# A graph network on one core: four groups instead of one per turn of TensorE's loop in the sparse sums

## The reference, cut to what matters

```python
# layer 0: ten hops
for _ in range(10):
    f = 0.9 * segment_sum(f[src] * edge_weight[:, None], dst, n) + 0.1 * feat_0
# layer 1: an edge network on [x[src], x[dst], edge_attr], averaged by destination
# layer 2: degree-normalised sum over edges, a linear layer
agg = segment_sum(x[src] * ci[src][:, None], dst, n) * cj[:, None]
# layer 3: symmetric-normalised sum with self loops, batch norm
agg = segment_sum(h[src] * norm[:, None], dst, n)
```

## Time and profile before

| | |
|---|---|
| median of 3 runs | 9797.47 us (9789.39 to 9800.16) |
| span of the profiled execution | 10,854.4 us (no other time was recorded for it) |
| TensorE matmuls busy | 8603.5 us, 79% of the span, 233,310 of them |
| VectorE busy | 7212.7 us, 66% |
| GpSimd busy | 5092.9 us, 47% |
| ScalarE busy | 4566.9 us, 42% |
| DMA | 1796 MB, mean 165 GB/s |
| packets of the DMA queue for instructions, q8 | 151, 2.47 MB |

### The profile page before, as it was taken

The page is one execution under the profiler, slowest core; times in us unless marked ns, Lnnn a source line. Parts: engine busy times, 40 slices in busy tenths (PEclk is TensorE's granted clock), DMA queues, the critical chain, the costliest instruction groups (busy, mean ns, idle before and its releaser), DMA issues. The chain is left out here.

```text
span 10854.4 us, 564438 instructions
## 1 busy us (share of the span) xinstructions
PE 8603.5 (79%) x233310; PEld 6985.0 (64%) x233310; DVE 7212.7 (66%) x17719; ACT 4566.9 (42%) x9489; POOL 5092.9 (47%) x4838
## 2 busy tenths in 40 slices
PE   5886776788989989889899894777777777759585
PEld 4665665778888888888888882343334333348585
DVE  7998987877777777777777773333333333367377
ACT  2332997954444444444444442333333333324132
POOL 0000000046767667667667674455555555537064
PEclk9998995589999999999999997888888888879598
DMA  3000005588988889889888893222222222249085
GB/s 28 0 0 0 0 0 186 226 278 282 303 280 287 297 283 302 280 282 302 282 287 297 282 302 80 53 57 56 52 53 56 55 54 54 54 138 303 21 289 178
DMA packets 548661, 1796.17 MB, mean 165 GB/s; under 512 B 210662, under 2 KB 272126, under 8 KB 546686
## 3 DMA queue, kind: packets, MB, share of 16 engines
q1 hardware_dynamic: 469374, 1740.04, 48.4%
q0 software_dynamic: 59776, 46.03, 2.8%
q10 hardware_dynamic: 19328, 7.36, 0.4%
HBM read 1628.31 MB, written 159.79 MB: 165 GB/s over the span
## 5 line engine op out<-in xcount | busy, mean ns | idle before, releaser
L1159 POOL TENSOR_TENSOR arena<-arena 128x768 f32<-128x768 f32 (+2 forms) x1800 | 2739.3, 1522 | 3965.3 <-DVE arena L1215 3922.5
L1128 ACT CAST arena<-banks 128x384 bf16<-128x384 f32 (+1 forms) x3600 | 1993.1, 608 | 2856.2 <-DVE banks L1211 2855.1
L1259 PE MATMUL banks<-arena 32*128 32x144 bf16 x118800 | 2359.3, 224 | 188.1 <-issue 173.1
L1247 PE MATMUL banks<-arena 128*128 128x48 bf16 x58800 | 2504.4, 184 | 2.7 <-issue 2.6
L1247 PEld LDWEIGHTS banks<-arena 128*128 128x128 fp8e4 x58800 | 2345.7, 96 | 6.7 <-issue 5.9
L1215 DVE TENSOR_TENSOR arena<-banks,arena 128x384 f32<-128x384 f32 (+1 forms) x3600 | 1931.2, 567 | 568.2 <-ACT arena L1128 568.2
L1247 PE MATMUL banks<-xc,arena 128*128 128x48 bf16 x24500 | 2063.6, 185 | 219.1 <-DVE arena L1186 59.7
L1504 POOL DMA_INDIRECT f<-node_table,idx x1568 | 1537.6, 981 | 1444.1 <-ACT idx L1512 979.2
L1247 PEld LDWEIGHTS banks<-xc,arena 128*128 128x128 fp8e4 x24500 | 1903.0, 96 | 415.4 <-issue 147.4
L1259 PEld LDWEIGHTS banks<-arena 32*128 32x128 bf16 x118800 | 1965.5, 92 | 315.0 <-issue 220.7
L1211 DVE TENSOR_TENSOR banks<-banks,wslot 128x384 f32<-128x384 f32 (+1 forms) x3600 | 1877.1, 567 | 366.8 <-PE banks L1247 363.2
(11 more groups left out here) (329 smaller groups left out, 11611.5 us busy)
## 6 DMA issues: line engine op xcount, KB each, us to landing
arena<-onehots SPq DMA_DIRECT2D x1200, 768.0 KB, 4.2
arena<-onehots SPq DMA_DIRECT2D x300, 864.0 KB, 4.4
arena<-onehots SPq DMA_DIRECT2D x300, 800.0 KB, 4.3
arena<-in_dst SPq DMA_DIRECT2D x195, 512.0 KB
onehots<-arena SPq DMA_DIRECT2D x100, 768.0 KB, 3.3
node_table<-xc SPq DMA_DIRECT2D x11, 2352.0 KB, 17.8
f<-node_table,idx POOLq DMA_INDIRECT x1568
onehots<-arena SPq DMA_DIRECT2D x25, 864.0 KB, 3.5
```

The costliest lines, as they stand in the source:

```text
L1128: m = nc.scalar.copy(as_bank(mp_b[:, b % 3, 0, tiles, :, 1]), bank)
L1159: nc.gpsimd.tensor_tensor(mp[:, b % 3, 2, 0:NTILE[b], :], mp[:, b % 3, 1, 0:NTILE[b], :], mp_b[:, b % 3, 1, 0:NTILE[b], :, 1], ALU.subtrac ...
L1247: m = nc.tensor.matmul(to, hot[:, i * P:(i + 1) * P], x_part, start=c == 0, stop=c == 2)
L1259: m = nc.tensor.matmul(banks[:, 4 + q, 0:3 * D], hot[rows, i * P:(i + 1) * P], mp_b[rows, b % 3, :, i, :, 1], start=b == 0 and i == 0, sto ...
```

## The change

TensorE's loop over the first 24 groups takes four groups in a turn, so that it has 6 turns and a body four times as long, written out. The order of the matmuls and waits is the same. The loops of the other engines keep one group per turn.

```diff
+PE_TURN = 4
...
+    assert (NGRP - 1) % PE_TURN == 0
...
-                    with pe.Fori(0, NGRP - 1) as d:
-                        for b in range(NBATCH):
-                            gather(d + (b + 2) // NBATCH, (b + 2) % NBATCH)
-                            scatter(d, b)
+                    with pe.Fori(0, (NGRP - 1) // PE_TURN) as t:
+                        for d in (t * PE_TURN + i for i in range(PE_TURN)):
+                            for b in range(NBATCH):
+                                gather(d + (b + 2) // NBATCH, (b + 2) % NBATCH)
+                                scatter(d, b)
```

## The result

The changed kernel takes 12,264 us (median of 4 runs, 12,224 to 12,272) against 9,797 us for the kernel before on the same chip. The ratio is 1.2511, with a 95% interval of 1.2496 to 1.2526. The prediction had the direction, the mechanism and the range (10,950 to 12,300); its middle, 11,550, was 714 us too low.

A forecast was written before the change was run, and what follows sets the result against it. TensorE was taken to bound the sums, DMA close behind. Fetching 276 groups (1,352 us) and 60 dearer branches (306 us) gave +1,660 us on 9,797; from three readings it took 11,550 us, range 10,950 to 12,300.

The forecast's parts named there:

- TensorE sets the pace, other engines are covered: Loop over groups in the sums: TensorE is busy 15.45 of 16.10 us a group; slower TensorE covers the others.
- DMA is close behind: Loop over groups: DMA is busy 92% of the 16.10 us turn, 14.8 us a group.
- the third reading to the measured time: Unprofiled loop already at its DMA limit of 14.8 us a group, fetches as long as ever: 11,816 us.
- A turn of before runs from held instructions, the rest is fetched: TensorE's loop: a turn of about 1,400 instructions needs no instruction packets; all other code is fetched, 256 instructions a packet.
- The change saves up to 0.9 us for each branch removed: TensorE's loop edge: 18 of 23 taken branches per sum go, 216 in all, at most 190 us gained.
- The rival in which fetching is hidden: TensorE's unrolled loop: blocks come in time, so the kernel gets 190 us faster, 9,610 us; chance 5%.
- The rival in which a part is kept: TensorE's unrolled loop: some 7 of 22 blocks are met again, +1,130 us, about 10,930; chance 5%.
- 5.46 periods of 3.85 us per group: TensorE's unrolled loop: 5.46 instruction blocks a group, one per period p, 21.0 us a group; 276 groups cost 1,352 us.
- A branch that stays costs 5.1 us more: TensorE's loop: 60 remaining branches jump to blocks not held, 3.6 us plus about 1.5 us each, 306 us.
- The rival with DMA or the clock as the bound: In the sums: packets queue behind one-hots, p 4.34 or more, +2,420 us, 12,220; or pauses lower the clock; chance 10%.
- The sum: Whole kernel: 1,352 us for fetched groups plus 306 us for remaining branches, +1,660 us.
- The three readings from the profile to the measured time: Whole kernel, from a profiled 10,854 to the median 9,797 us: same ratio 11,295, same addition 11,457, or DMA-limited loop 11,816.

The follow-up runs named there:

- experiment 10: Kernel before, with SyncE's loop fetching only 64 columns of each batch of one-hots: 9,765 us against 9,803 on that chip.
- experiment 5: Kernel before with 120 more one-column matmuls per turn of TensorE's loop, a body of about 1,640 instructions: 13,731 us against 10,832 on that chip.
- experiment 9: Kernel with the 1,640-instruction body, plus 48 matmuls ahead of TensorE's loop in each copy of the sum: 10,640 us against 9,803 for before.
- its second form: Kernel with the 1,640-instruction body, with 27 instead of 48 matmuls ahead of the loop in each copy: 11,968 us against 10,852 for before.
- experiment 3: Changed kernel with two groups per turn instead of four: 12,654 us, ratio 1.292 to the kernel before.
- experiment 6: Kernel before with 360 more one-column matmuls per turn of TensorE's loop, a body of about 2,120 instructions: 17,659 us.
- experiment 1: The kernel before, unedited, profiled again: 9,795 us, span 9,793.
- experiment 7: Changed kernel with all 24 groups in one turn, no branch taken back: 12,753 us, ratio 1.178 to 10,832 on that slow chip.
- Experiment 4: Changed kernel, with SyncE's loop fetching only 64 columns of each batch of one-hots: 11,622 us, 642 us less than the changed kernel.
- experiment 8: Kernel before with all 25 groups in TensorE's loop, no last group behind it: 10,820 against 10,832 us (slow chip), 9,753 against 9,803 (quick chip).

## Why the prediction was right, and where its sizes were off

*TensorE sets the pace, other engines are covered*: right. The only waits of its loads in the changed turn are for its own sequencer. *DMA is close behind*: wrong as a bound, by experiment 10. It did no harm to the sum, but the third reading to the measured time rested on these 14.8 us, and they bound nothing.

*A turn of before runs from held instructions, the rest is fetched*: right, and now sharper. What decides is how many blocks of 256 the loop touches. By the places of the stalls (an estimate from counted instructions) the loop touches 7, 6 and 6 blocks in the three copies of before; 8, 7 and 7 in experiment 5; 7, 7 and 7 in experiment 9; 7, 8 and 8 in its second form. Every copy with 7 or fewer was held in all turns; at 8, some six turns in ten were fetched; longer bodies (experiments 3 and 6, the change) were fetched in every turn. The places were fitted to the first three kernels afterwards; for the last one they were worked out ahead, and all three copies came out as they say. The Trainium skill (Runtime: NRT & Kernel Launch, section Instruction fetch mechanics) gives TensorE room for 2,048 instructions, 8 blocks. The runs agree if the block behind the loop, fetched ahead, takes one of them, and a fetched turn at 8 blocks did bring 9 packets; still, that is argued, not shown, and why some turns at 8 blocks are held stays open.

*The change saves up to 0.9 us for each branch removed*: too much. Two thirds of it was the stall of 0.6 us, which the faster chip doesn't have (experiment 1). The rival in which fetching is hidden is out, by experiments 3 and 7: the blocks came late with 2, 4 and 24 groups in a turn. The Trainium skill's sentence that kernels prefer full unrolling (Runtime: NRT & Kernel Launch, section Instruction fetch mechanics) doesn't hold here: with all 24 groups written out the kernel is 18% slower than before on the same chip. The rival in which a part is kept is out as well: 24 packets a turn for 21.8 blocks.

*5.46 periods of 3.85 us per group*: the right count, and the right period for an empty DMA. Experiment 4's turns, 88.9 us on average, are almost exactly what the prediction's terms give, 4 x 21.0 + 5.1 = 89.1. With the one-hots they are 98.0 us. This is the term that was mis-sized: p under load was about 4.2 us (4.15 between single stalls; 4.25 by whole turns, (98.0 - 5.1) / 21.8), nearer to the 4.34 of the earlier trace rows than to the 3.88 of the earlier trace rows. The prediction had named the load and taken 3.85, below the middle of its bounds. *A branch that stays costs 5.1 us more*: right, 5.0 by experiment 3 (5.8 by experiment 7, 350 us over 60, across the two kinds of chip), though the branch itself takes 4.85 us instead of 3.6. The packets, 1,788 against the 1,660 predicted, are 24 a turn and not 21.8: each turn fetches about two blocks more than its own length.

*The rival with DMA or the clock as the bound*, given 10%, had the number: 12,220 us against 12,264. Of its mechanism a half came true: p rose to about 4.2 with the one-hots' traffic, but the one-hots were not late, since no wait of the turn names them. Of the clock, which the prediction kept at 1.00 by the earlier trace rows, the changed turn shows 0.90, so that argument failed; what it cost is not shown. Nor does a run show whether all instruction packets go through one DMA engine, the reason given for leaving out the low end of p.

*The sum*: predicted +1,660 us, measured +2,472 in the sums. Of the 812 us missing, 276 x 0.72 = 199 are the group of before, which was 15.38 us on a quick chip and not 16.10. About 613 are turns of 98 instead of 89 us. *The three readings from the profile to the measured time* asked what the profiler adds. It adds nothing that shows (spans of 12,266.6 and 9,793 us beside times of 12,268 and 9,795 for the same executions), and the gap of 1,057 us is no effect of profiling: against experiment 1's trace, 869 us of it lie in the edge network and 192 in the sums, as on the slow chips of experiments 7 and 8. What could have been asked is in which stage a span was 10% longer than the time.

*The range* reached 12,300 us, and the time lies 36 us below that. There is luck in this: without the third reading's 359 us, which rested on the DMA bound that experiment 10 refutes, the sum's highest end would have been 12,220.

## What to carry to other kernels

A loop body that TensorE still holds when it jumps back costs nothing to fetch; one a little longer costs a fetch for every 256 instructions, and TensorE with small matmuls ran through 256 in 2.7 to 2.9 us here while a block came every 3.8 to 4.2 us on average. Count the instructions of a TensorE loop before unrolling it, including where it begins in its block, and look for the instruction queue in windows of the loop: no packets, or several a turn. The same view shows the gain that is to be had: code around the loop that repeats (a peeled last group) may push the whole out of what is held, and rolling it back in brought 0.5% here, on a quick chip.

## What the runs showed of the hardware that was not expected

- 54 or 96 instructions placed ahead of a loop, without any wait changed, took it from 27.8 to 18.5 us a turn or the other way (experiments 5 and 9).
- A loop at the edge of what is held doesn't settle: turns of 18 and of 34 us follow in no fixed order, and in none of 12 such sums did two of 18 us follow each other (experiments 5 and 9).
- The DMA share of a stretch can be 0.95 without bounding it: with 0.08 the turn stayed at 15.38 us (experiment 10).
- Chips differ by 10% on this kernel: 0.7 us in each turn of TensorE's loop, most of it a stall 3.2 us behind each branch that the others don't have the earlier trace rows (with the longer held body of experiment 9 the turns differ by only 0.2 us, 18.55 against 18.3), and about 3,100 against 2,247 us in the edge network. Why is open.
